# Where a batch's feature statistics are computed: VectorE between the picks, or ScalarE in the late loop

## What is computed

```python
h = max(layernorm(x), 0)                        # over the 128 channels, eps 1e-5
idx = the first 25 neighbours of each node (by index)
agg = max over these neighbours of h[idx]       # with 0 too, where the node has 25 or fewer
out = x + relu(concat([h, agg]) @ W + b)
```

## Time and profile before

| | before |
|---|---|
| median of 3 runs | 659.41 us (658.31 to 660.83) |
| the profiled execution | 659.89 us |
| its span, first to last instruction | 658.2 us |
| mean granted TensorE clock, share of full speed | 0.983 |
| late rounds, all 16 groups | 43 (344 pairs of matmuls at 8 a round) |

### The profile page before, as it was taken

How to read it: one execution, slowest core, us unless ns; L and a number is a source line. 1 busy time by engine, 2 the same in 40 slices (tenths; PEclk the granted TensorE clock), 3 DMA queues, 4 the chain that set the end, 5 groups by cost and what they waited for, 6 DMA issues and landing times.

```text
span 658.2 us, 9830 instructions
## 1 busy us (share of the span) xinstructions
PE 589.7 (90%) x2800; PEld 255.4 (39%) x2800; DVE 595.3 (90%) x731; ACT 400.2 (61%) x552; POOL 96.1 (15%) x142
## 2 busy tenths in 40 slices
PE   4578989899999999899998999899998999999886
PEld 2223434343434434344443434344443434443322
DVE  4965979999898999999999999999999998989996
ACT  3346827767486746958477666958477664836210
POOL 1400006000060002400060002400060000600000
PEclk9968989999999999999999999999999999999999
DMA  8745875858359583567558484557558362240100
GB/s 336 230 128 206 323 191 209 224 173 245 84 197 227 193 241 132 186 157 259 158 211 239 161 259 158 191 151 278 136 215 235 100 197 52 85 157 19 61 16 17
DMA packets 99438, 115.81 MB, mean 176 GB/s; under 512 B 66003, under 2 KB 85718, under 8 KB 94934
## 3 DMA queue, kind: packets, MB, share of 16 engines
q1 hardware_dynamic: 98262, 114.46, 55.3%
q10 hardware_dynamic: 1152, 1.05, 0.5%
HBM read 58.85 MB, written 20.97 MB: 121 GB/s over the span
## 4 chain that ended last, share of the span: by engine, by line
PE 32%; issue 29%; DVE 23%; POOL 6%; ACT 4%; DMA 3%; SPq 2%; DVEq 1%; POOLq 0%; ACTq 0%
PE picked L640 10%; PE picked L641 9%; DVE best L829 9%; PE ring L569 5%; DVE late_hot L841 4%; DVE best L835 3%; POOL h L400 2%; PE final L667 2%; PE final L671 2%; DVE hot L816 2%; DMA late_skew<-late 1%; POOL h L394 1%; POOL h L397 1%; ACT late L480 1%; PE side L598 1%
## 5 line engine op out<-in xcount | busy, mean ns | idle before, releaser
L829 DVE TENSOR_TENSOR best<-picked,best 128x1024 f32<-128x1024 f32 x224 | 269.9, 1217 | 24.6 <-PE picked L641 23.8
L640 PE MATMUL picked<-hot,h_hi 128*128 128x512 f16 x512 | 196.2, 383 | 11.5 <-DVE best L835 6.8
L641 PE MATMUL picked<-hot,h_lo 128*128 128x512 f16 x512 | 195.7, 382 | 0.0
L640 PE MATMUL picked<-late_hot,hi_skew 128*128 128x512 f16 x344 | 130.5, 379 | 25.3 <-DVE best L829 12.7
L641 PE MATMUL picked<-late_hot,lo_skew 128*128 128x512 f16 x344 | 130.4, 379 | 0.0
L835 DVE TENSOR_TENSOR best<-picked,best 128x1024 f32<-128x1024 f32 x86 | 105.0, 1221 | 15.4 <-PE picked L641 14.9
L467 ACT ACTIVATE late_rank<-ring,late_bias 128x512 bf16<-128x512 f32 x128 | 81.6, 686 | 58.9 <-PE ring L569 58.9
L475 ACT ACTIVATE chosen<-side,bias_cut 128x512 bf16<-128x512 f32 x120 | 82.5, 688 | 47.3 <-PE side L598 47.3
L467 ACT ACTIVATE rank<-ring,late_bias 128x512 bf16<-128x512 f32 x120 | 81.8, 682 | 16.1 <-PE ring L569 16.1
L498 ACT COPY best<-picked 128x1024 f32<-128x1024 f32 x32 | 32.4, 1014 | 87.3 <-PE picked L641 87.3
L640 PEld LDWEIGHTS picked<-hot,h_hi 128*128 128x128 f16 x512 | 50.2, 98 | 85.8 <-DVE best L829 15.5
(11 more groups left out here) (89 smaller groups left out, 488.4 us busy)
## 6 DMA issues: line engine op xcount, KB each, us to landing
adj_in<-in_adj_dram SPq DMA_DIRECT2D x15, 2048.0 KB, 8.4
picks<-kept SPq DMA_DIRECT2D x15, 1024.0 KB, 5.0
kept<-chosen SPq DMA_DIRECT2D x112, 128.0 KB, 3.0
late_skew<-late SPq DMA_DIRECT2D x32, 192.0 KB, 3.6
x_in<-in_x_dram SPq DMA_DIRECT2D x8, 512.0 KB, 6.3
late_skew<-late SPq DMA_DIRECT2D x16, 256.0 KB, 4.8
late_skew<-late SPq DMA_DIRECT2D x32, 128.0 KB, 3.6
xres<-in_x_dram SPq DMA_DIRECT2D x16, 256.0 KB, 2.7
```

Source lines behind the costliest of these rows:

```text
L640: nc.tensor.matmul(dst, hi[:, slot, k, :], onehot, start=start, stop=False)
L641: return nc.tensor.matmul(dst, lo[:, slot, k, :], onehot, start=False, stop=stop)
L829: nc.vector.tensor_tensor(best[:, half, s, :, :], picked[s][:, :, :], best[:, half, s, :, :], ALU.max).then_inc(picked_read, 1)
```

## The change

For batches 1 to 7 the statistics move to ScalarE, into `spreads`: eight `Copy` activations with scale -1/128, each of which also writes its row sum, give minus the mean; eight `Square` activations with that as bias, again with row sums, give the sum of squares off the mean; the square root then divides by 128 and adds the eps. The elementwise results go to `h32` and are not used. Two waits on ScalarE's own signals are added, and waits for the load of `x` and for `lo_made`. VectorE's `stats_of` and `moments_of` remain for batch 0. GpSimd adds minus the mean where it subtracted the mean.

```diff
-    STATS_USES, MOMENTS_USE, GAIN_USE = (9, 10), 12, 5
+    GAIN_USE = 5
...
+        minus_mean = sb("minus_mean", [P, K], F32)
+        squares = sb("squares", [P, K], F32)
...
-                mean = moments[:, :, 0:1].to_broadcast([P, K, C])
-                nc.gpsimd.tensor_tensor(h32[:, :, :], x_in[:, :, :], mean, ALU.subtract).then_inc(centred, 1)
+                if isinstance(batch, int) and batch == 0:
+                    mean = moments[:, :, 0:1].to_broadcast([P, K, C])
+                    nc.gpsimd.tensor_tensor(h32[:, :, :], x_in[:, :, :], mean, ALU.subtract).then_inc(centred, 1)
+                else:
+                    mean = minus_mean[:, :].unsqueeze(2).to_broadcast([P, K, C])
+                    nc.gpsimd.tensor_tensor(h32[:, :, :], x_in[:, :, :], mean, ALU.add).then_inc(centred, 1)
...
             def spreads(batch):
-                act.wait_ge(moments_made, K * batch + K)
-                nc.scalar.activation(spread[:, :], moments[:, :, 1], ACT.Sqrt, bias=bias_eps[:, 0:1]).then_inc(spread_made, 1)
+
+                act.wait_ge(x_loaded, 16 * batch + 16)
+                act.wait_ge(lo_made, batch)
+                for k in range(K):
+                    nc.scalar.activation(h32[:, k, :], x_in[:, k, :], ACT.Copy, scale=-1.0 / C,
+                                         accum_out=minus_mean[:, k:k + 1]).then_inc(means_made, 1)
+                act.wait_ge(means_made, K * batch)
+                for k in range(K):
+                    nc.scalar.activation(h32[:, k, :], x_in[:, k, :], ACT.Square, bias=minus_mean[:, k:k + 1],
+                                         accum_out=squares[:, k:k + 1]).then_inc(squares_made, 1)
+                act.wait_ge(squares_made, K * batch)
+                nc.scalar.activation(spread[:, :], squares[:, :], ACT.Sqrt, bias=bias_eps[:, 0:1], scale=1.0 / C).then_inc(spread_made, 1)
...
                 for use in range(PAIRS, USES):
                     t, p = use // PAIRS, use % PAIRS
                     take_pair(g, use, s)
...
-                    if use in STATS_USES and ahead:
-                        half = STATS_USES.index(use)
-                        stats_of(batch_of(it, u) + 1, range(half * HALF, (half + 1) * HALF))
-                    if use == MOMENTS_USE and ahead:
-                        moments_of(batch_of(it, u) + 1)
```

More of the change, by code:

```diff
@@ L204, in build @@
         moments_made = sem("moments_made")
+        means_made = sem("means_made")
+        squares_made = sem("squares_made")
         spread_made = sem("spread_made")
@@ L481, in find_late, with first_spreads @@
                                      bias=bias_late[:, 0:1]).then_inc(late_made, 1)
+            def first_spreads():
+                act.wait_ge(moments_made, K)
+                nc.scalar.activation(spread[:, :], moments[:, :, 1], ACT.Sqrt, bias=bias_eps[:, 0:1]).then_inc(spread_made, 1)
             def spreads(batch):
-                act.wait_ge(moments_made, K * batch + K)
-                nc.scalar.activation(spread[:, :], moments[:, :, 1], ACT.Sqrt, bias=bias_eps[:, 0:1]).then_inc(spread_made, 1)
+                act.wait_ge(x_loaded, 16 * batch + 16)
[9 more added lines that the diff above has]
+                nc.scalar.activation(spread[:, :], squares[:, :], ACT.Sqrt, bias=bias_eps[:, 0:1], scale=1.0 / C).then_inc(spread_made, 1)
             def turned_h(batch, slot, n):
@@ L510, in _ @@
                 if k == 1:
-                    spreads(0)
+                    first_spreads()
                 act.wait_ge(chosen_made, k + 1)
@@ L794, in first_low, with first_stats, first_moments @@
                 nc.vector.tensor_tensor(h_lo[:, 0, :, :], h32[:, :, :], h_hi[:, 0, :, :], ALU.subtract).then_inc(lo_made, 1)
-            def stats_of(batch, classes):
-                dve.wait_ge(x_loaded, 16 * batch + 16)
-                for k in classes:
+            def first_stats():
+                dve.wait_ge(x_loaded, 16)
+                for k in range(K):
                     nc.vector.bn_stats(stats[:, k, :], x_in[:, k, :]).then_inc(stats_made, 1)
-            def moments_of(batch):
-                dve.wait_ge(stats_made, K * (batch + 1))
+            def first_moments():
+                dve.wait_ge(stats_made, K)
                 nc.vector.memset(held[:, 3:4], 0.0)
@@ L871, in _ @@
                 nc.vector.tensor_copy(mask_t[:, 2 * n:2 * n + 2, :], turned_bank[n]).then_inc(block_copied[1], 1)
-            stats_of(0, range(K))
-            moments_of(0)
+            first_stats()
+            first_moments()
             make_gain(0)
@@ L920, in step @@
                 more = not at_end(it, u, 1)
-                ahead = u % PER_BATCH == 0 and not at_end(it, u, PER_BATCH)
                 for use in range(PAIRS, USES):
```

## The result

| | before | after |
|---|---|---|
| median of 10 runs | 659.19 us (657.68 to 660.83) | 661.50 us (660.73 to 664.18) |
| the profiled execution | 659.89 us | 660.96 us |
| its span | 658.2 us | 659.2 us |

A forecast was written before the change was run, and what follows sets the result against it. TensorE was taken as the bound beside the uses, VectorE only at the late loop's entry. Gains of 1.0 us in four-round groups less 0.4 lost in three-round ones gave -0.5 us from 659.89: 659.4 us, range 656.5 to 667.5.

The forecast's parts named there:

- The rest, at nothing: Waits for `lo_made` and the load of `x`, GpSimd's addition, DMA, `gain` and square-root table loads: priced at no cost.
- What bounds the kernel, VectorE's spare time: Beside the uses TensorE is the bound, every 1.51 us; VectorE has 0.38 us to spare in each use.
- VectorE's saving, 0.32 us in 7 groups: Late loop's entry: its first maximum and TensorE's wait on that chain come 0.32 us earlier per group, 2.2 us in all.
- The block, 5.9 us: ScalarE's sixteen added activations, two waits and the root, between masks and first copy: 5.9 us per group.
- free room of 5.79: ScalarE before the next copies in three-round groups: the block costs nothing up to 5.79 us, beyond it one for one.
- The wait for `late_rank`: TensorE's wait for ScalarE's first `late_rank` instruction behind the copies: 0.18 us, to stay as before.
- The sum: Whole kernel: 1.0 us back in three four-round groups, 0.4 lost in four three-round groups, -0.5 us, giving 659.4 us.
- The rivals: Outgrown room 0.27, `Square` table loads 0.04, VectorE's time counting for more (653 us) 0.06, no change 0.63.
- the block didn't outgrow its room: Rival at the second copy in three-round groups: row sums as second instructions, block 7.3 us, total 665 us; chance 0.27.
- no table load in the loop: Rival in ScalarE's block: `Square` outside the root's table, two loads of 1.283 us per block, total 670 us; chance 0.04.
- "slower": Whole kernel slower by more than 0.5% (3.3 us), from outgrown room or table loads; chance 0.31.
- Against a rule: Skill's rule keeps simple arithmetic on VectorE; 2.1 us removed there, about 5.9 added on ScalarE, slower once room is spent.

The follow-up runs named there:

- padded kernels: Kernel before with 34, 16 or 8 one-column ScalarE copies behind the root of each batch's first group: 662.24, 662.46, 663.16 us (1.0046, 1.0051, 1.0044).
- Experiment 3: Kernel before without VectorE's statistics of batches 1 to 7, batch 0's values used for all: 657.49 us, 0.998.
- experiment 4: Changed kernel with ScalarE's eight copies and eight squares each in a hardware loop of two passes of four: 664.13 us, 1.0071.
- Experiment 5: Changed kernel with ScalarE's loop over the groups written out, other engines keeping theirs: 659.23 us, 0.9988.
- its control: Kernel before with ScalarE's loop over the groups written out in the same way: 659.02 us, 0.9988.
- experiment 8: Changed kernel, ScalarE's loop written out, root behind the third `late_rank`, TensorE's round-count read ahead of use 15's transposes: 658.30 us, 0.9984 to before.

## Why the prediction was wrong

The step that failed is "The rest, at nothing": it priced signals, loads of data, GpSimd and tables, and left out the loading of ScalarE's own instructions. That cost some 1.6 and 1.8 us at the two returns of the changed kernel, and in the padded kernels, where nothing else is changed, 1.6 to 2.0 us at each, 3.4 to 3.6 in all by the periods and 2.9 to 3.4 by the ratios. The trace of before could have warned: q14 stops loading after the loop's first pass, so the body fitted; by how much, no row told. The Trainium skill, "Runtime: NRT & Kernel Launch", in "Instruction fetch mechanics", says that an engine's instruction memory is a small FIFO with sequential prefetch, and that a taken branch to a target outside the pages held forces a fetch before execution goes on. The traces agree for the bodies of 282 and more, which are loaded again in every pass and stand 2.5 to 2.8 us at the return; of the body of 266 they show no load in the later passes. So the step was there to be asked about, though not its price.

- *What bounds the kernel, VectorE's spare time:* right. Without statistics VectorE waits 0.29 us in use 13.
- *VectorE's saving, 0.32 us in 7 groups:* right in its mechanism and too high on the mean. Experiment 3 shows 0.12 on the mean of six groups. I had left TensorE's first late matmul where it was; it is held by the reading of the round count, so that it comes 1.27 us behind the transposes or up to 0.7 more from case to case, and then it eats the saving. With that read moved (and the root) the saving is 0.34 on the mean of six.
- *The block, 5.9 us:* right, 5.89. Its free room of 5.79: right to 0.1 us, since the three-round groups lost 0.03 to 0.06 where 0.11 was forecast, and half a us with the block longer (experiment 4). The wait for `late_rank`, forecast as before, grew from 0.18 to 0.47 us in the three-round groups.
- *The sum:* -0.5 us without the stalls. Experiment 5 has 0.9988, with 1 in its interval, and its control the same. With the stalls' 3.4 us the sum would have been +2.9, where the medians have +2.3, the ratio +3.2 and the periods together +2.5.
- *The rivals:* the block didn't outgrow its room, and there was no table load in the loop. The time of 661.5 lies inside the range, and below the 0.5% of "slower". That is luck: the kernel moved the other way than forecast, for a reason that no rival named.
- *Against a rule:* VectorE lost 2.1 us a group and ScalarE took on 5.9. The extra work was hidden, so the rule's outcome did not come by its own way.

## What to carry to other kernels

An instruction moved to another engine also moves into that engine's loop body. Count the instructions from branch to branch on each engine, sums as instructions of their own, and look whether its instruction queue is silent in later passes; if it is, a few more can cost a wait at every return. When an engine is relieved, look at every other thing that releases the next instruction, the reading of a register too: the saving ends at the next latest one. And before an instruction is moved within its engine, look at who waits for its signal in another queue, since there it holds up all that stands behind it.

## What the runs showed of the hardware

- A ScalarE loop body of 266 recorded instructions returned to its start in 0.25 us; bodies of 282, 298 and 334 took 2.5 to 2.8 us, with no trend in their size. From one return to the next the first moved no packet on the instruction queue q14, the others five of 8 KB each. Written out without a loop, the same work had no such gap.
- `accum_out` on a 128x128 activation is a second instruction of 0.19 us, of which 0.10 us adds to the engine's time.
- Loading the round count into a TensorE register took 0.30 us on the median and up to 1.36. With the instructions around it, it left TensorE idle for 0.6 to 1.3 us before the first late matmul in the groups of the table (experiments 3 and 5, before and after). With the read ahead of four transposes (experiment 8), nothing of that idle time was left in the six groups.
